# A vision-tower layer on one core: x normalised by halves, the scales' store on another queue, Wo in two halves, and edits at both ends

## The reference, cut to what matters

```python
# 1. mixing: an S4D kernel; dt = exp(log_dt), A = -exp(inv_A_real) + 1j*A_imag
dtA = A * dt[:, None]
Cc  = B * x * (exp(dtA) - 1) / A                      # x plays C
K   = 2 * einsum('chn,hnl->chl', Cc, exp(dtA[:, :, None] * arange(1024))).real    # (32, 128, 1024)
h   = concat([cls_tok, K], axis=1)                    # 129 rows of 1024
# 2. causal attention on layernorm(h): 32 query heads, 8 key/value heads of 32, rotary q and k
h   = h + attn(layernorm(h)) @ Wo.T
# 3. feed-forward on layernorm(h), both operands rounded to 8 bits (scale per token, per channel)
h   = h + fq(layernorm(h)) @ fq(w).T + b
```

## Time and profile before

| | |
|---|---|
| median of three runs | 1557.4 us (1556.73 to 1558.63) |
| the profiled execution, own time | 1555.19 us |
| its span, first to last instruction | 1553.4 us |
| PE busy | 1455.2 us, 94% |
| DVE busy | 1302.5 us, 84% |
| ACT / POOL busy | 770.2 us, 50% / 798.9 us, 51% |
| mean granted clock of TensorE | 0.978 of full speed |

### The profile page before, as it was taken

How to read it: one execution, slowest core, us unless ns; L and a number is a source line. 1 busy time by engine, 2 the same in 40 slices (tenths; PEclk the granted TensorE clock), 3 DMA queues, 4 the chain that set the end, 5 groups by cost and what they waited for, 6 DMA issues and landing times. The chain is left out here.

```text
span 1553.4 us, 34419 instructions
## 1 busy us (share of the span) xinstructions
PE 1455.2 (94%) x10754; PEld 1136.2 (73%) x10786; DVE 1302.5 (84%) x2354; ACT 770.2 (50%) x2711; POOL 798.9 (51%) x744
## 2 busy tenths in 40 slices
PE   5899898999999999999999999669999999999996
PEld 3899776777777777777777777556777777777774
DVE  8888677989889898888989888658988888888875
ACT  8796465676666667666666666541111111111110
POOL 0895135676676666667576676323333333333333
PEclk8899999999999999999999999889999999999998
DMA  9356526777777677776767776863333232332321
GB/s 230 103 137 156 166 79 131 203 194 199 199 198 207 190 195 197 199 205 192 201 194 195 196 202 178 273 175 117 114 116 109 94 122 89 114 109 93 122 79 37
DMA packets 220106, 244.90 MB, mean 158 GB/s; under 512 B 30001, under 2 KB 158130, under 8 KB 220050
## 3 DMA queue, kind: packets, MB, share of 16 engines
q1 hardware_dynamic: 214290, 223.14, 50.8%
q10 hardware_dynamic: 5760, 21.04, 4.5%
HBM read 138.29 MB, written 106.57 MB: 158 GB/s over the span
## 5 line engine op out<-in xcount | busy, mean ns | idle before, releaser
L1166 ACT ACTIVATE pr<-sm,ml 128x128 f32<-128x128 f32 x1024 | 398.9, 392 | 154.1 <-DVE ml L1339 153.6
L924 POOL TENSOR_TENSOR pr<-pr,ri 128x512 f32<-128x512 f32 x256 | 266.2, 1040 | 251.3 <-DVE ri L1346 245.4
L1017 PE MATMUL att_ps<-w_lo,xT_hi 128*128 128x512 f32 x792 | 326.7, 412 | 0.0
L1017 PE MATMUL att_ps<-w_hi,xT_hi 128*128 128x512 f32 x792 | 319.5, 403 | 0.0
L1017 PE MATMUL att_ps<-w_hi,xT_lo 128*128 128x512 f32 x792 | 314.4, 397 | 0.0
L1323 DVE STREAM_TRANSPOSE pB<-pr 128x512 f32<-128x512 f32 x256 | 177.1, 692 | 59.7 <-POOL pr L924 36.5
L1623 PE MATMUL ffn_o<-wo_hi,cT_hi 128*128 128x512 f32 x528 | 215.7, 409 | 3.6 <-ACT wo_hi L1653 2.5
L1623 PE MATMUL ffn_o<-wo_hi,cT_lo 128*128 128x512 f32 x528 | 207.1, 392 | 0.0
L1623 PE MATMUL ffn_o<-wo_lo,cT_hi 128*128 128x512 f32 x528 | 205.9, 390 | 0.0
L1330 DVE TENSOR_TENSOR sm<-att_ps,cst 128x512 f32<-128x512 f32 x256 | 169.0, 660 | 29.3 <-PE att_ps L1078 29.3
L1166 ACT ACTIVATION_READ_ACCUMULATOR pr<-sm,ml 128x1 f32 x1024 | 193.4, 189 | 0.0
(11 more groups left out here) (205 smaller groups left out, 2386.0 us busy)
## 6 DMA issues: line engine op xcount, KB each, us to landing
pT<-p_blocks SPq DMA_DIRECT2D x256, 256.0 KB, 2.8
p_blocks<-pB SPq DMA_DIRECT2D x512, 64.0 KB, 2.0
h_rows<-ho SPq DMA_DIRECT2D x64, 256.0 KB, 4.1
ctx_turned<-ctxo SPq DMA_DIRECT2D x64, 256.0 KB, 3.3
h_in<-h_rows SPq DMA_DIRECT2D x32, 512.0 KB, 4.3
out_dram<-yo SPq DMA_DIRECT2D x32, 512.0 KB, 2.7
ctx_in<-ctx_turned SPq DMA_DIRECT2D x30, 512.0 KB, 3.6
hbuf<-h_rows ACTq DMA_DIRECT2D x29, 512.0 KB, 4.7
```

Of the source, the lines that this page charges most:

```text
L924: G.tensor_tensor(pr[:, g % 4], pr[:, g % 4], ri[:, g % 2, :].unsqueeze(2).to_broadcast([P, GQ, P]), ALU.mult).then_inc(p_ready, 1)
L1017: mm = nc.tensor.matmul(bank[:], x_part[:, t[1], e, tok:tok + P], w_part[blk][:, e, :], start=(r == 0), stop=(r == EC * 3 - 1))
L1166: a = nc.scalar.activation(pr[:, g % 4, q, :], sm[:, g % 2, q, :], ACT.Exp, bias=ml[:, b[1], 0, h:h + 1], accum_out=ml[:, b[1], 1, h:h + 1])
```

## The change

1. **x by halves.** `normalise(n, r)` does 512 columns. GpSimd does half 0 at step 3 and half 1 at step 5, each behind that step's `normalise_p`; `rope_sum(t, 0)` stays at step 4. `turn_x(n, r)` waits for its own half, and the other counts of `xn_ready` are doubled. The tile of last rows is normalised in two halves too, by VectorE.
2. **The store of W's scales** goes from the start of tile 2 on SyncE's queue to step 4 of tile 2 on ScalarE's.
3. **Wo.** Half 0 is loaded where both were; half 1 in tile 32, step 0, on ScalarE's queue, behind `load_first` and ahead of the wait of `split_first`.
4. **The start.** GpSimd does the first round's multiply-adds and three small operations of the denominator; VectorE keeps the whole part and the subtraction, further down its order. ScalarE does the first two sines before any copy, four copies, the sine table and magnitudes of the slots, and then the rest of the copies of x, each followed by two first-round magnitudes. TensorE does four swaps, the turning of `dup`, and the other four swaps. The first half's coefficients are made pair by pair (two channels at a time), each released to TensorE by itself; the copy of `ident_b` moves behind them, and `whole(1)` behind the second half's coefficients.
5. **The end.** For the last tile GpSimd's `hb` waits for `f_xn`, and the last `yo` is added by VectorE in two halves, each behind its scaling.

```diff
     TURNS = [("x", i) for i in range(R_SMALL)] + [("small", 0)] + [("x", i) for i in range(R_SMALL, XR)] + \
-            [("swap", i) for i in range(XR)]
+            [("swap", i) for i in range(OUT_BANKS)] + [("g", i) for i in range(G_TURNS)] + \
+            [("swap", i) for i in range(OUT_BANKS, XR)]
+    COPIED = [turn for turn in TURNS if turn[0] != "g"]
...
@@ mixing, GpSimd
+        pool.wait_ge(decays, 1)
+        nc.gpsimd.tensor_tensor(den[:], o["x"][:, 0:NS], o["x"][:, 0:NS], ALU.mult).then_inc(den_link, 1)
+        nc.gpsimd.tensor_tensor(te[:], aim[:], aim[:], ALU.mult).then_inc(den_link, 1)
+        pool.wait_ge(den_link, 2)
+        nc.gpsimd.tensor_tensor(den[:], den[:], te[:], ALU.add).then_inc(den_ready, 1)
+        pool.wait_ge(turned_out, R_SMALL + 2)
+        for h in range(CP):
+            t = nc.gpsimd.tensor_scalar(yb[:, 0, h, :], iota, rates[:, 1, h:h + 1], quarter, ALU.mult, ALU.add)
+        t.then_inc(phases, 1)
...
@@ mixing, ScalarE
-        for r in range(XR + 1):
-            copy_round(r)
         act.wait_ge(for_act, 1)
         nc.scalar.activation(s1[:], ta[:], ACT.Sin).then_inc(sines, 1)
         nc.scalar.activation(s2[:], ta[:], ACT.Sin, scale=0.5).then_inc(sines, 1)
+        for r in range(R_SMALL + 1):
+            copy_round(r)
...
+        act.wait_ge(turned_out, R_SMALL + 1)
+        for r in range(R_SMALL + 1, XR + 1):
+            copy_round(r)
+            magnitudes(0, 2 * (r - R_SMALL - 1), 2)
+        for i in range(OUT_BANKS):
             copy_round(XR + 1 + i)
-            magnitudes(0, 2 * i, 2)
+        magnitudes(0, CP - 6, 6)
         sine(0)
+        for i in range(OUT_BANKS, XR):
+            copy_round(XR + 1 + i)
         magnitudes(1, 0, CP)
@@ mixing, VectorE
-        v.wait_ge(turned_out, XR + 1)
-        turns_of(0)
...
-        link(V.tensor_tensor(den[:], a, a, ALU.mult))
-        link(V.tensor_tensor(s1[:], aim[:], aim[:], ALU.mult))
-        link(V.tensor_tensor(den[:], den[:], s1[:], ALU.add))
+        v.wait_ge(den_ready, 1)
...
+        v.wait_ge(phases, 1)
+        V.tensor_scalar(kb[:], yb[:, 0], MAGIC, -MAGIC, ALU.add, ALU.add).then_inc(wholes, 1)
+        v.wait_ge(wholes, 1)
+        V.tensor_tensor(yb[:, 0], yb[:, 0], kb[:], ALU.subtract).then_inc(fracs, 1)
...
+        def first_coefficients(i):
+            for part, (own, term) in enumerate(((c1, m1), (c2, m2))):
+                t = V.tensor_tensor(
+                    term[:, 0, 2 * i:2 * i + 2], own[:, 2 * i:2 * i + 2, :].unsqueeze(2).to_broadcast([P, 2, JB, NB]),
+                    g_ps[:, part, :, 2 * i:2 * i + 2].rearrange("p j h -> p h j").unsqueeze(3)
+                    .to_broadcast([P, 2, JB, NB]), ALU.mult)
+            t.then_inc(first_products, 1)
...
-        v.wait_ge(turned, ROUNDS)
-        v.wait_ge(turned_out, len(TURNS))
-        coefficients(0, 0)
+        v.wait_ge(turned, TURNS.index(("g", G_TURNS - 1)) + 1)
+        v.wait_ge(turned_out, XR + 2)
+        for i in range(PAIRS):
+            first_coefficients(i)
+        v.wait_ge(first_products, PAIRS)
+        V.tensor_copy(ident_b[:], ident).then_inc(products, 1)
+        coefficients(0, 1)
         whole(1)
-        coefficients(0, 1)
@@ attention, GpSimd
-        def normalise(n):
-            G.tensor_scalar(xn[:], hbuf[:, n[1], :], mv[:, 0:1], rstd[:], ALU.subtract, ALU.mult
+        def normalise(n, r):
+            cols = slice(r * BK, (r + 1) * BK)
+            G.tensor_scalar(xn[:, cols], hbuf[:, n[1], cols], mv[:, 0:1], rstd[:], ALU.subtract, ALU.mult
                             ).then_inc(xn_ready, 1)
...
                 if s == 3 and has_rows(n) and not last_rows(n):
-                    normalise(n)
+                    normalise(n, 0)
...
+                if s == 5 and has_rows(n) and not last_rows(n):
+                    normalise(n, 1)
@@ attention, TensorE
-            pe.wait_ge(xn_ready, nth(n) + 1)
+            pe.wait_ge(xn_ready, XROUNDS * nth(n) + r + 1)
@@ attention, ScalarE
+                if s == 4 and at(t, 2):
+                    act.wait_ge(w_scaled, EC // 2)
+                    with nc.allow_non_contiguous_dma(reason="1024 scales"):
+                        act.dma_start(scale_dram.rearrange("a (t p) -> (a p) t", p=P), wsc[:]
+                                      ).then_inc(scales_out, 16)
...
                     load_first(act)
+                    load_wo(act, (1,))
                     split_first(act)
...
-                    load_wo(act)
+                    load_wo(act, (0,))
@@ feed-forward, GpSimd and VectorE
+                if last_rows(t):
+                    pool.wait_ge(normed, u + 1)
                 nc.gpsimd.tensor_tensor(hb[:, t[1], :], h1[:, t[1], :], bias_sb[:], ALU.add).then_inc(biased, 1)
...
+        def add_last(c, half):
+            u = number(c)
+            cols = slice(half * BK, (half + 1) * BK)
+            v.wait_ge(biased, u + 1)
+            v.wait_ge(scaled, 2 * u + half + 1)
+            v.wait_ge(out_stored[c[1]], 16 * c[0])
+            done = V.tensor_tensor(yo[:, c[1], cols], ya[:, c[1], cols], hb[:, c[1], cols], ALU.add)
+            if half == 1:
+                done.then_inc(last_ready, 1)
```

More of the change, by code:

```diff
@@ L372, in tensor @@
         pe.wait_ge(cst_loaded, 32)
-        for r, (kind, i) in enumerate(TURNS):
+        for kind, i in TURNS:
+            if kind == "g":
+                if i % (G_TURNS // 2) == 0:
+                    pe.wait_ge(turn_in, 2 + 2 * i // G_TURNS)
+                for q in range(4):
+                    part, slot = divmod(4 * i + q, JB)
+                    mm = nc.tensor.transpose(g_ps[:, part, slot, :],
+                                             dup[:, 4 * i + q].rearrange("h n r -> h (n r)"), ident)
+                mm.then_inc(turned, 1)
+                continue
+            r = COPIED.index((kind, i))
             if kind == "x":
@@ L395, in tensor @@
             mm.then_inc(turned, 1)
-        for i in range(G_TURNS):
-            if i % (G_TURNS // 2) == 0:
-                pe.wait_ge(turn_in, 2 + 2 * i // G_TURNS)
-            for q in range(4):
-                part, slot = divmod(4 * i + q, JB)
-                mm = nc.tensor.transpose(g_ps[:, part, slot, :],
-                                         dup[:, 4 * i + q].rearrange("h n r -> h (n r)"), ident)
-            mm.then_inc(turned, 1)
-        pe.wait_ge(turned_out, len(TURNS))
+        pe.wait_ge(turned_out, len(COPIED))
         for k in range(NCP):
@@ L1282, in normalise_last_rows @@
             rows = slice(0, NB)
-            V.tensor_scalar(xn[rows], hbuf[rows, n[1], :], mv[rows, 0:1], rstd[rows], ALU.subtract, ALU.mult
-                            ).then_inc(xn_ready, 1)
+            for r in range(XROUNDS):
+                cols = slice(r * BK, (r + 1) * BK)
+                V.tensor_scalar(xn[rows, cols], hbuf[rows, n[1], cols], mv[rows, 0:1], rstd[rows],
+                                ALU.subtract, ALU.mult).then_inc(xn_ready, 1)
         def split_x(n, r):
@@ L1532, in load_first @@
     def load_first(sp):
-        sp.wait_ge(xn_ready, NB + 1)
+        sp.wait_ge(xn_ready, 2 * (NB + 1))
         sp.wait_ge(x_turned, 2 * NB + 2)
@@ L1872, in body @@
                 quantise(t)
-            if exists(c, NT):
-                scale_out(c, 0)
-                scale_out(c, 1)
+            for half in range(2):
+                if exists(c, NT):
+                    scale_out(c, half)
+                if last_rows(c):
+                    add_last(c, half)
             if at(t, 1):
@@ L1942, in load_qkv, with load_wo @@
                                  .rearrange("(q d) e -> d q e", d=DH)).then_inc(raw_in[b], 16)
-        def load_wo(sp):
-            for b in range(2):
+        def load_wo(sp, halves):
+            for b in halves:
                 sp.dma_start(sbuf["wo_raw"][:, 4 * b:4 * b + 4, :],
```

52 lines of the change are left out of this document (24 added, 28 removed).

## The result

The changed kernel takes 1545.5 us (median of 4 runs), the kernel before 1557.1 in the same session: ratio 0.9924, 95% interval 0.9907 to 0.9941. Measured once more it was 1543.9 against 1557.5, ratio 0.9916 (0.9903 to 0.9930). So it is 12 to 13 us faster, where 30 were forecast, and slower than 1542, the upper end of the range. The profiled execution has a span of 1542.8 us.

The account below looks back on a forecast made before the run. TensorE was taken to set the pace of steady attention, 3% idle. Gains 15.5 + 0.4 + 4.5 + 4.5 + 2.0 + 3.3 = 30.2 us from the profiled 1555.2 gave 1525.0, or 1527 against the median; range 1514 to 1542.

Parts of the forecast that it names:

- Item 1: Steady tiles, x by halves: the wait before `turn_k` goes, 0.25 us appears at `turn_x`; 0.5 a tile, 15.5 us gained.
- 31 tiles that wait: Attention tiles: the count by which the 0.5 us gained per tile was multiplied, first ones included, giving 15.5 us.
- rival A: Steady tiles: the wait only changes hands, to `xT_lo` or `pB`'s DRAM writes; 0.1 us a tile gained, time 1539.5; chance 0.16.
- Item 2: Tile of last rows, normalised in two halves: `turn_x` starts after the first half; 0.4 us gained, bounds 0 and 0.4.
- Item 3: Tile 2, store of the scales moved to ScalarE's queue: 4.5 us gained of the store's 6.3, bounds 0 and 6.3.
- on ScalarE's queue at step 4 it has nothing urgent behind it: Tile 2, store of the scales: the reason given for moving it; it supports the 4.5 us gain.
- rival B: Scales' store and Wo's second half: shared engines, same harm elsewhere, both give nothing; 21.2 us gained, time 1536; chance 0.17.
- Item 4: Tiles 31 and 32, Wo by halves: shorter burst gains 6.5 us, second half loses 2; 4.5 gained, bounds -1 and 7.
- Item 5: Start, first-round multiply-adds moved from VectorE to GpSimd: coefficients ready earlier; 2.0 us gained, bounds -0.5 and 3.
- as `whole(1)` with its 2.62 wait no longer stands ahead: Start: why the second half's coefficients would be ready by 47.2, part of the 2.4 us gained before ScalarE's 0.4.
- TensorE is without gaps afterwards: After the start: why the start's gain of 2.0 us would be carried through the mixing.
- Item 6: End, faster last `f_xn` (2.0 us) and last sum split on VectorE (1.7 to 1.8): 3.3 gained, between 2.5 and 3.8.

Follow-up runs that it names:

- e15: The changed kernel unaltered, measured and profiled a second time: 1543.9 us against 1557.5, ratio 0.9916.
- e1: The changed kernel with the store of the scales issued again by SyncE at the start of the same tile: 1541.2 us, ratio 0.9900.
- e10: The kernel before with only the store of the scales moved to ScalarE's queue at step 4 of the same tile: 1559.7 us against 1557.8, ratio 1.0004.
- e6: The changed kernel with the store of the scales issued by SyncE in tile 1, as soon as they are ready: 1535.0 us, ratio 0.9860.
- e9: The changed kernel with the store at its new place but written as 128 pieces of 32 bytes (output scaled wrongly, same work): 1534.7 us, ratio 0.9843.
- e16: The kernel before with only Wo loaded in two halves, the second behind the feed-forward's loads: 1555.8 us against 1557.5, ratio 0.9988.
- e2: The changed kernel with both halves of Wo loaded at once in tile 31, as before the change: 1548.9 us, ratio 0.9943.
- e14: The kernel before unaltered, run once more for a second profile; no time given, stretch E 79.0 us.
- e3: The changed kernel with `whole(1)` put back ahead of the second half's coefficients: 1542.9 us, ratio 0.9905.
- e4: The changed kernel without any of the start's edits: 1543.1 us, ratio 0.9903.
- e8: The changed kernel with Wo's second half loaded two steps later, at step 2 of tile 32: 1546.3 us, ratio 0.9928.
- e11: The changed kernel with the store in tile 1, `whole(1)` ahead again and the first context tile loaded in tile 31: 1532.3 us, ratio 0.9834.

## Why the prediction was wrong

By stretches the changed kernel's gain, on the means of the profiles, is: 30 tiles of 0.485 = 14.6; start -1.0 (A, 211.6 to 212.7); last rows' tile 0.6 (A, 212.2 before, 211.6 with the halves); store -4.2 (6.5 to 10.7); stretch E -0.9 (78.4 to 79.3); end 2.5 (F, 22.7 to 20.2). Together 11.6. The means of A, B - 3C and E are good to some 0.3 to 0.9 us each. Of the 18.6 us that are missing from 30.2, the store makes 8.7, halves of x and Wo together 6.3 (5.9 in stretch E, 0.4 in the thirty tiles), the start 3.0, the end 0.8; the last rows' tile gave 0.2 more than forecast.

**Item 1, right in 30 tiles, wrong in the last.** The mechanism, the next wait and its size (0.5 a tile) came as argued. (The 0.75 of the working divides the 12.8 us of a 400 us stretch by the 17 tiles of one of 416; by its own stretch it is 0.78, which changes nothing.) But the step "31 tiles that wait" counted tile 31 like the others, and there rival A's mechanism holds. In the changed kernel, VectorE, TensorE and SyncE's queue, and last the same place of SyncE's queue in the kernel before:

```profile
...
950.49 0.71 DVE L1358 STREAM_TRANSPOSE pB<-pr 128x512 f32<-128x512 f32 x1 [1.32 <-DMA p_blocks<-pB]
...
954.37 0.65 DVE L1323 TENSOR_TENSOR xT_lo<-att_ps,xT_hi 128x512 fp32r<-128x512 f32 x1
...
955.12 0.63 PE L1076 MATMUL att_ps<-cst,xn 128*128 128x128 f32 x4 [2.29 <-issue]
...
941.76 3.78 SPq L867 DMA_DIRECT2D p_blocks<-pB  x4
```

```profile
...
950.72 3.06 SPq L839 DMA_DIRECT2D p_blocks<-pB  x4
```

`pB` waits 1.32 us for its blocks' writes and `xT_lo` and `turn_x` follow, 2.29 us late; the `pB` before it had already waited 1.51 us (1.34 in e15's profile, ended by a block's write). D is 24.8 in the four profiles with whole `xn` and 26.9 on the mean of fourteen with halves: 2.1 longer instead of 0.5 shorter. That it is the writes is read from the traces. Why just here: SyncE takes 2.9 to 4.0 us to issue one group of four block writes, some 5 us ahead of `turn_k` of tile 30, in all eighteen profiles, of the kernel before too, and never over 1.95 in tiles 6 to 29. With whole `xn` the slack nearly covered it, with halves it doesn't. Tile 30 is the first that is written out behind the loop over the steady ones; what holds the queue there no run shows.

These 2.1 us are a part of stretch E. The whole of it, with Wo loaded at once, is 78.4 with whole `xn` (three profiles) and 82.9 with halves (two), so the halves of x lose some 4.5 of their 14.6 us there, and Wo in halves gives 3.6 of them back (79.3). Against 15.5 and 4.5 forecast, 5.4 of the 6.3 missing are thus of item 1 and 0.9 of item 4.

**Item 2, right in kind.** The 0.6 is within the scatter of A. In the two traces the first `xT_lo` starts 2.35 us after `xn` does where it was 2.62, 0.3 for the 0.4 forecast.

**Item 3, wrong in its sign.** The step that failed is "on ScalarE's queue at step 4 it has nothing urgent behind it". That is a statement on the issuing queue. What the store holds up is the other queue's blocks on the shared engines, and in the 10 us after 256 us there are blocks of two groups on their way. The earlier trace rows showed it: a DMA of 4 KB that cost 6.3 us can't be one of size. The lower bound of 0 left out that the new place may be worse, as it was: by 4.2 on the means of the profiles, by 2.5 to 3.7 in the times at the new pace (e1), by nothing sure at the old one (e10). With the store out of the way or in 128 pieces 9 to 10 us come out (e6, e9), more than the 6.3 that it was priced at. These runs agree with the rule quoted from the Trainium skill ("DMA: Bandwidth & Descriptors", "Issuing engines are not separate DMA queues"): another issuer changed nothing for the better (e10), another time did (e6). I had rival B for it at 0.17, priced at nothing gained, not as a loss.

**Item 4, right in kind, its size too large.** TensorE's gap shrank to 1.58 us as forecast ("1 or 2"). But the gap is not the end of the chain: 1.9 us come out alone (e16), 3 to 4 beside the halves of x (e2). After that gap most of TensorE's waiting in this stretch ends with VectorE's `wo_lo` (13.2 of some 22 us in e16, 11.1 of some 21 in the changed kernel); that this swallows the gain is read, not tried. And the baseline was one profile in which the context tile came early (e14).

**Item 5, wrong by one step.** The first product came at 42.3, where 42.6 was forecast, at full clock, and VectorE was released at 49.84, where 49.8 was forecast. The failed step is "as `whole(1)` with its 2.62 wait no longer stands ahead": I counted what its going back gives to the coefficients, and not who waits for `whole(1)`: GpSimd's subtraction, its sixteen phases and the next round's whole part. With it in the old place the start gives 1.6 on the means of A (211.6 to 210.0), close to the 2.0 forecast; the times don't show it (0.9905 in e3, 0.9903 in e4 without the start's edits). "TensorE is without gaps afterwards" was true of the kernel before only.

**Item 6, right in kind, 0.8 too high.** `f_xn` takes 0.81 instead of 2.82 and the last sum 0.69, as forecast, but `xr`, now beside `hb`, 1.36 where without GpSimd it took 0.75: 0.6 lost. The trace agrees there with the rule that the prediction quotes from the Trainium skill ("SBUF — State Buffer", section "SBUF: two separate sides") and priced at 0.5. The prediction had 0.45 set aside for it. The rest is 0.5 that it did not name: the last tile's 16 products take 5.93 us instead of 5.41, at a granted clock of 0.61 where it was 0.66.

That it would be faster was right. The time lies outside the range since two terms fell below their lower bounds (the store's 0, measured -4.2; the start's -0.5, measured -1.0, which the scatter doesn't tell from -0.5) in the same kernel in which halves of x and Wo gave 6.3 less than forecast, nearly all of it in stretch E.

## What to carry to other kernels

A DMA is placed by what else is moving and what is due in the next 10 us, not by whose queue is free; and many single values are to be made few pieces, or moved to a quiet stretch. When an operation is moved back behind another, list who waits for it before counting what the other gains. A gain per tile of a loop is to be checked in the tiles outside the loop's steady state, where other transfers run; and a baseline that is one profile is good to no better than the scatter of its waits for DMAs, here 2 to 3 us in a stretch.

## What the runs showed of the hardware

- 4 KB as 1024 values of 4 bytes took 9.7 us to land beside other traffic and 5.9 in a quiet stretch; as 128 pieces of 32 bytes at most 5.0 beside the same traffic, and it cost nothing that could be seen. The 1040 packets of the single values themselves took only some 0.5 to 0.6 us of the 16 engines' time. In the changed kernel they were over by 260 us, and it was in the 5 us after them that the engines were 0.61 busy at 36 GB/s with the other queue's packets, at 0.25 us each instead of 0.05; with the old pace (e10) it was 0.95 busy at 81 GB/s in the same 5 us.
- Wo's 4 MB cost least in four loads: E 82.9 as one (two profiles with the halves of x), 79.3 as two halves (eight, without e8 and e11), 75.3 as four quarters (74.2 with the first context tile loaded early too). All these are with the halves of x.
- A wait of TensorE that the profile ends with nothing ("issue") was in truth one for VectorE's `xT_lo`: it ended 0.1 us after that did, in tile 31 of the changed kernel and of e2.
- SyncE took some 1.8 us, at most 1.95, to issue four block writes in tiles 6 to 29, and 2.9 to 4.0 in one place ahead of `turn_k` of tile 30, in all eighteen profiles.
